# One tile pair per half head: a relu of a score difference on ScalarE, its add and maximum in one VectorE operation

## The reference

```python
mod = (_silu(L0_c) @ L0_wmod).reshape(L0_c.shape[0], 6, 1, -1)
h = _layernorm(x) * (1 + ca) + sa
q = ((h @ W_q + b_q) @ W_s)            # into heads of 16 columns
k, v = h @ W_k + b_k, h @ W_v + b_v
scores = einsum('bhqd,bhkd->bhqk', q, k) / sqrt(16)
out = einsum('bhqk,bhkd->bhqd', softmax(scores), v)
x = x + ga * (out @ W_o + b_o)
h = _layernorm(x) * (1 + cb) + sb
x = x + gb * ffn(h)                    # 8 experts, each takes its 512 best tokens
```

## Time and profile before

| | |
|---|---|
| median of three runs | 1736.55 us (1734.66 to 1736.87) |
| profiled execution | span 1734.7 us; mean granted TensorE clock 0.979 |
| attention's exponentials | 131 to 1397 us |
| a unit | 19.6 us in the even stretch |
| busy over the span | TensorE 97%, VectorE 87%, ScalarE 74%, GpSimd 13% |
| reduces of groups (L230) | 1024, 1191.6 us busy |
| exponentials (L1080) | 2048, 1079.4 us busy |
| group matmuls (L223), score matmuls (L584) | 2048 each |
| PV matmuls (L1139) | 10752 |

### The profile page before, as it was taken

The page is one execution under the profiler, slowest core; times in us unless marked ns, Lnnn a source line. Parts: engine busy times, 40 slices in busy tenths (PEclk is TensorE's granted clock), DMA queues, the critical chain, the costliest instruction groups (busy, mean ns, idle before and its releaser), DMA issues. The chain is left out here.

```text
span 1734.7 us, 43731 instructions
## 1 busy us (share of the span) xinstructions
PE 1685.5 (97%) x17251; PEld 969.8 (56%) x17251; DVE 1513.5 (87%) x1908; ACT 1291.7 (74%) x2454; POOL 229.3 (13%) x300
## 2 busy tenths in 40 slices
PE   8999999999999999999999999999999998599998
PEld 5645555555555555555555554555555586488887
DVE  5678999999999999999999999999999476687774
ACT  2327888888888888888888888888888834365663
POOL 0422012100010000001000000100000012135433
PEclk9999999999999999999999999999999997599999
DMA  8660443222222223323222223342220331235332
GB/s 265 207 178 24 92 98 53 41 41 39 52 55 39 41 49 52 47 40 65 41 42 39 39 41 54 59 60 39 41 42 12 108 107 61 98 101 143 89 82 37
DMA packets 93658, 122.03 MB, mean 70 GB/s; under 512 B 24060, under 2 KB 70716, under 8 KB 90348
## 3 DMA queue, kind: packets, MB, share of 16 engines
q1 hardware_dynamic: 84492, 109.22, 28.1%
q0 software_dynamic: 6144, 8.39, 2.7%
q10 hardware_dynamic: 2816, 1.61, 0.3%
HBM read 79.35 MB, written 38.54 MB: 68 GB/s over the span
## 5 line engine op out<-in xcount | busy, mean ns | idle before, releaser
L230 DVE TENSOR_REDUCE pmax<-ps 128x2 f32<-128x1024 f32 x1024 | 1191.6, 1215 | 54.2 <-PE ps L223 50.2
L1080 ACT ACTIVATE pt<-ps 128x512 f32<-128x512 f32 x2048 | 1079.4, 600 | 179.8 <-PE ps L584 157.7
L223 PE MATMUL ps<-kp,qp 48*128 48x512 f32 x2048 | 622.4, 458 | 2.9 <-DVE pmax L230 2.9
L1139 PE MATMUL ps<-pt,v_st 128*32 128x256 f32 (+1 forms) x10752 | 589.7, 334 | 0.7 <-ACT pt L1080 0.7
L584 PE MATMUL ps<-qp,kp 50*128 50x512 f32 x2048 | 560.8, 422 | 0.5 <-ACT pt L1080 0.5
L584 PEld LDWEIGHTS ps<-qp,kp 50*128 50x128 f32 x2048 | 292.5, 185 | 265.2 <-ACT pt L1080 263.1
L1139 PEld LDWEIGHTS ps<-pt,v_st 128*32 128x32 f32 x10752 | 265.7, 109 | 261.0 <-issue 187.2
L223 PEld LDWEIGHTS ps<-kp,qp 48*128 48x128 f32 x2048 | 245.6, 184 | 108.1 <-issue 89.8
L213 POOL CAST m_parts<-rowmax_t 128x32 fp32r<-128x32 f32 x64 | 13.5, 211 | 864.5 <-DVE rowmax_t L247 864.5
L1752 PE MATMUL ps<-w_l,hid_h 128*128 128x256 f32 x256 | 72.3, 283 | 0.0
L446 ACT ACTIVATE pt<-ps,xb 128x512 fp32r<-128x512 f32 x32 | 21.8, 687 | 64.7 <-PE ps L613 63.7
(11 more groups left out here) (229 smaller groups left out, 1297.6 us busy)
## 6 DMA issues: line engine op xcount, KB each, us to landing
kp<-k_parts SPq DMA_DIRECT2D x186, 128.0 KB, 4.5
v_all<-L_ffn_w SPq DMA_DIRECT2D x16, 1024.0 KB, 6.9
qp<-q_parts SPq DMA_DIRECT2D x186, 64.0 KB, 4.1
k_parts<-pt SPq DMA_DIRECT2D x16, 512.0 KB, 3.4
q_parts<-pt SPq DMA_DIRECT2D x16, 512.0 KB, 2.9
o_rows<-o_sb SPq DMA_DIRECT2D x64, 128.0 KB, 3.4
sums_c<-o_rows SPq DMA_DIRECT2D x512, 0.5 KB
m_rows<-m_parts SPq DMA_DIRECT2D x256, 2.0 KB
```

Of the source, the lines that this page charges most:

```text
L223: last = nc.tensor.matmul(slot[:, half * CH:(half + 1) * CH], qp[rows, r, a * P:(a + 1) * P], kp[rows, r, c * CH:(c + 1) * CH], start=True ...
L230: v.reduce_max(pmax[:, u % 2, 2 * k:2 * k + 2], slot.rearrange("p (f t) -> p f t", f=2), AX.X).then_inc(groups_out, 1)
L1080: nc.scalar.activation(pt[:, s % PTS, half * CH:(half + 1) * CH], bank(n % SCORE_BANKS), ACT.Exp, scale=SCALE).then_inc(scores_out, 1)
L1139: last = mm(acc[32 * j:32 * (j + 1), first * QB:(first + many) * QB], v_st[:, h % NBUF, kt, :], probs[:, :, j * QB:(j + 1) * QB], start=kt ...
```

## The change

For the units 2 to 61 (`folds`), the key chunks 2 and 3 of the last query tile (groups 14 and 15) are treated in another way. Group 14 is not made. TensorE makes instead, for each of the two halves, the difference of the two chunks' scores, in a bank of the score ring: queries times chunk 2, then, accumulated onto it, negated queries times chunk 3 (`fold_scores`). ScalarE writes the relu of that difference to `fold` (`take_fold`). Group 15 is filled as before with chunk 3's scores; VectorE adds the relu to them, which gives the larger of the two chunks' scores, and takes the maximum over the row in the same operation (`tensor_tensor_reduce`), one for each half.

The two fold products of unit u stand in the scores of unit u-1, ahead of its chunks 5 (low rows, block 1) and 6 (high rows, block 2). They take places in the ring of three banks (`RING`, `FOLD_RING`), so a unit has 34 places for 32. GpSimd negates the query tile (`negate_queries`) behind the split of the maxima of the unit before. Block 5 issues one group where it issued two, so that there are 15 in a unit. Waits that counted groups or chunks count by the new lists.

```diff
+LOWEST = -3.0e38
+FOLD_TILE, FOLD_FROM, FOLD_END = KT // NCH - 1, 2, UNITS - 2
+FOLD_K = FOLD_TILE * NCH + NCH - 1
+FOLD_PLACES = (5, 6)
+def folds(u):
+    return FOLD_FROM <= u < FOLD_END
+GROUPS = [(u, k) for u in range(UNITS) for k in range(KT) if not (folds(u) and k == FOLD_K - 1)]
+FOLD_BEFORE = {(u - 1) * UNIT_CHUNKS + at: (u, half) for u in range(FOLD_FROM, FOLD_END) for half, at in enumerate(FOLD_PLACES)}
+RING, FOLD_RING = [], {}
+for chunk in range(UNITS * UNIT_CHUNKS):
+    if chunk in FOLD_BEFORE:
+        FOLD_RING[FOLD_BEFORE[chunk]] = len(RING) + len(FOLD_RING)
+    RING.append(len(RING) + len(FOLD_RING))
...
+        q_minus = sb("q_minus", [P, P], F32R)
+        fold = stage_b[:, 0, :].rearrange("p (h t) -> p h t", h=2)
...
         def reduce_group(dve, v, n, slot):
-            u, k = divmod(n, KT)
+            u, k = GROUPS[n]
             dve.wait_ge(groups_full, n + 1)
-            v.reduce_max(pmax[:, u % 2, 2 * k:2 * k + 2], slot.rearrange("p (f t) -> p f t", f=2),
-                         AX.X).then_inc(groups_out, 1)
+            if folds(u) and k == FOLD_K:
+                if u < FOLD_FROM + 2:
+                    v.memset(pmax[:, u % 2, 2 * k - 2:2 * k], LOWEST)
+                for half in range(2):
+                    dve.wait_ge(scores_out, FOLD_RING[u, half] + 1)
+                    last = v.tensor_tensor_reduce(fold[:, half, :], slot[:, half * CH:(half + 1) * CH], fold[:, half, :],
+                                                  1.0, LOWEST, ALU.add, ALU.max,
+                                                  accum_out=pmax[:, u % 2, 2 * k + half:2 * k + half + 1])
+                last.then_inc(groups_out, 1)
+            else:
+                v.reduce_max(...)
...
+        def fold_scores(pe, u, half):
+            h, f = divmod(u, HALVES)
+            at, a = FOLD_RING[u, half], f * (QT // 2) + FOLD_TILE
+            rows = slice(HALF * half, HALF * half + KROWS)
+            pe.wait_ge(q_negated, u - FOLD_FROM + 1)
+            pe.wait_ge(scores_out, at - SCORE_BANKS + 1)
+            nc.tensor.matmul(ring_bank(at), qp[rows, h % NBUF, a * P:(a + 1) * P],
+                             kp[rows, h % NBUF, 2 * CH:3 * CH], start=True, stop=False)
+            nc.tensor.matmul(ring_bank(at), q_minus[rows, :],
+                             kp[rows, h % NBUF, 3 * CH:4 * CH], start=False, stop=True).then_inc(scores_full, 1)
+        def negate_queries(pool, g, u):
+            h, f = divmod(u, HALVES)
+            r, a = h % NBUF, f * (QT // 2) + FOLD_TILE
+            pool.wait_ge(operands_in[r], (h // NBUF + (r > 0)) * 16 * loads_of_head)
+            pool.wait_ge(parts_made, u)
+            if u > FOLD_FROM:
+                pool.wait_ge(scores_full, FOLD_RING[u - 1, 1] + 1)
+            for half in range(2):
+                rows = slice(HALF * half, HALF * half + KROWS)
+                links["pool"](g.tensor_scalar(q_minus[rows, :], qp[rows, r, a * P:(a + 1) * P].bitcast(F32), -1.0, None, ALU.mult))
+            pool.sem_inc(q_negated, 1)
         def scores(pe, s, half):
+            at = RING[n]
-            if n >= SCORE_BANKS:
-                pe.wait_ge(scores_out, n - SCORE_BANKS + 1)
+            if at >= SCORE_BANKS:
+                pe.wait_ge(scores_out, at - SCORE_BANKS + 1)
...
                     split_maxima(pool, g, u)
+                    if folds(u + 1):
+                        negate_queries(pool, g, u + 1)
...
+                def take_fold(u, half):
+                    act.wait_ge(scores_full, FOLD_RING[u, half] + 1)
+                    if u > FOLD_FROM:
+                        act.wait_ge(groups_out, GROUP_OF[u - 1, FOLD_K] + 1)
+                    nc.scalar.activation(fold[:, half, :], ring_bank(FOLD_RING[u, half]), ACT.Relu).then_inc(scores_out, 1)
                 for n in range(STEPS * 2):
+                    if n in FOLD_BEFORE:
+                        take_fold(*FOLD_BEFORE[n])
...
                     twice = b != DELAY and (b == 0 or b > DELAY and b % 2 == 1) or block == 2 * DELAY
+                    if b == BLOCKS // 2 and block > BLOCKS:
+                        twice = False
                     for n in range(many):
                         if n == (0 if twice or b == DELAY else 1) and group < len(GROUPS):
                             next_group(group)
                             group += 1
+                        if chunk in FOLD_BEFORE:
+                            fold_scores(pe, *FOLD_BEFORE[chunk])
                         scores(pe, *divmod(chunk, 2))
                         chunk += 1
```

More of the change, by code:

```diff
@@ L68 @@
 GATHER_SPARE = 14
+LOWEST = -3.0e38
[5 more added lines that the diff above has]
+GROUPS = [(u, k) for u in range(UNITS) for k in range(KT) if not (folds(u) and k == FOLD_K - 1)]
+GROUP_OF = {at: n for n, at in enumerate(GROUPS)}
+FOLD_BEFORE = {(u - 1) * UNIT_CHUNKS + at: (u, half) for u in range(FOLD_FROM, FOLD_END) for half, at in enumerate(FOLD_PLACES)}
[4 more added lines that the diff above has]
+    RING.append(len(RING) + len(FOLD_RING))
 class Link:
@@ L227, in reduce_group @@
         def reduce_group(dve, v, n, slot):
-            u, k = divmod(n, KT)
+            u, k = GROUPS[n]
             dve.wait_ge(groups_full, n + 1)
-            v.reduce_max(pmax[:, u % 2, 2 * k:2 * k + 2], slot.rearrange("p (f t) -> p f t", f=2),
-                         AX.X).then_inc(groups_out, 1)
+            if folds(u) and k == FOLD_K:
[8 more added lines that the diff above has]
+            else:
+                v.reduce_max(pmax[:, u % 2, 2 * k:2 * k + 2], slot.rearrange("p (f t) -> p f t", f=2),
+                             AX.X).then_inc(groups_out, 1)
             if k == 0 and u > 0:
                 join_maxima(dve, v, u - 1)
-            if n == STEPS - 1:
+            if n == len(GROUPS) - 1:
                 join_maxima(dve, v, u)
         def join_maxima(dve, v, u):
-            dve.wait_ge(groups_out, (u + 1) * KT)
+            dve.wait_ge(groups_out, GROUP_OF[u, KT - 1] + 1)
             if u > 0:
@@ L294, in adaln_moe_block @@
             GROUPS_OF[n] = ("u0", "u1", "u2", "u3", "t", "v0", "v1")
-        scores_full, scores_out = sem("scores_full"), sem("scores_out")
+        scores_full, scores_out, q_negated = sem("scores_full"), sem("scores_out"), sem("q_negated")
         def group_at(n, place):
@@ L569, in project_dve, with ring_bank @@
                     normalise(n + 2)
+        def ring_bank(at):
+            return bank(at % SCORE_BANKS)
+        def fold_scores(pe, u, half):
[19 more added lines that the diff above has]
+            pool.sem_inc(q_negated, 1)
         def scores(pe, s, half):
@@ L580, in scores @@
                 pe.wait_ge(low_done, chunks * 4 - 1)
-            if n >= SCORE_BANKS:
-                pe.wait_ge(scores_out, n - SCORE_BANKS + 1)
+            if at >= SCORE_BANKS:
+                pe.wait_ge(scores_out, at - SCORE_BANKS + 1)
             rows = slice(HALF * half, HALF * half + MROWS)
-            nc.tensor.matmul(bank(n % SCORE_BANKS), kp[rows, h % NBUF, kt * P:(kt + 1) * P],
+            nc.tensor.matmul(ring_bank(at), kp[rows, h % NBUF, kt * P:(kt + 1) * P],
                              qp[rows, h % NBUF, f * CH:(f + 1) * CH], start=True, stop=True).then_inc(scores_full, 1)
@@ L837, in project_rows @@
                 pe.wait_ge(xb_ready, 2 * NB)
-                pe.wait_ge(groups_out, STEPS)
+                pe.wait_ge(groups_out, len(GROUPS))
                 pe.wait_ge(normalised, G // HG // NB * HALVES)
@@ L933, in load_next @@
                 def load_next(g):
-                    sp.wait_ge(scores_full, (g + 1) * HALVES * KT * 2)
+                    sp.wait_ge(scores_full, RING[(g + 1) * HALVES * UNIT_CHUNKS - 1] + 1)
                     if g == 0:
@@ L1078, in _ @@
                         act.wait_ge(pv_done, blocks_until(n - 2 * PTS))
-                    act.wait_ge(scores_full, n + 1)
-                    nc.scalar.activation(pt[:, s % PTS, half * CH:(half + 1) * CH], bank(n % SCORE_BANKS),
+                    act.wait_ge(scores_full, RING[n] + 1)
+                    nc.scalar.activation(pt[:, s % PTS, half * CH:(half + 1) * CH], ring_bank(RING[n]),
                                          ACT.Exp, scale=SCALE).then_inc(scores_out, 1)
@@ L1091, in invert @@
                     inverse(v, f).then_inc(inverse_made, 1)
-                for n in range(EARLY_GROUPS, STEPS):
-                    u, k = divmod(n, KT)
+                for n in range(EARLY_GROUPS, len(GROUPS)):
+                    u, k = GROUPS[n]
                     done = u - 3
@@ L1131, in weigh @@
                     ready = chunks_of(block)
-                    pe.wait_ge(scores_out, ready[-1] + 1)
+                    pe.wait_ge(scores_out, RING[ready[-1]] + 1)
                     for s in sorted({n // 2 for n in ready}):
@@ L1153, in _ @@
                     twice = b != DELAY and (b == 0 or b > DELAY and b % 2 == 1) or block == 2 * DELAY
+                    if b == BLOCKS // 2 and block > BLOCKS:
```

(7 more changed lines are left out.)

## The result

The changed kernel takes 1801.66 us in the median of four runs (1800.21 to 1802.63), the one before 1736.01 (1734.66 to 1736.87): ratio 1.0384, 95% interval 1.0368 to 1.0399. It is slower by 65.7 us; 1804 was forecast. The profiled execution's span is 1800.8 us, 66.1 more. The sums carry differences and don't change by it.

The account below looks back on a forecast made before the run. TensorE and ScalarE, handing each other three PSUM banks, set the pace, not VectorE. Slots and bank waits sum to 1.15 us per unit, 69 us in 60 units, on 1734.7: 1803.7, said as 1804 (range 1758 to 1824).

Parts of the forecast that it names:

- PV behind the short block: PV matmuls after the block of chunks 6 and 7, where the second fold stands, come 1.20 us late.
- PV behind block 3: PV matmuls after the block of chunk 10, which waits for chunk 7's bank, come 1.39 us late.
- VectorE worth nothing: VectorE's two reduces become two adds with maximum, 0.8 us less busy per unit; worth nothing on the path.
- ScalarE's Relu at 0.49: Each of the two new 128x512 Relus per unit on ScalarE takes 0.49 us, as exps do start to start.
- Three slots more, one less: On TensorE, folds add three matmul slots per unit, block 5 loses one: two of 0.24, 0.48 us at least.
- The ring: Among three score banks, chunk 5 waits for chunk 3's exp, chunk 10 for chunk 7's: 0.67 us per unit beyond slots.
- Halves that overtake: On TensorE, chunk 6 may run beside the second fold's first product, one slot earlier: nothing or 14 us less.
- GpSimd: Negating the query tile twice per unit takes 0.3 us each, with cover of over 8 us before the fold.
- Rival 1: Only TensorE's added matmul slots cost time: 0.48 x 60 = 29 us, 1764; chance 0.15.
- Rival 2: Three matmuls in a row on one half leave TensorE's weight loads unhidden: 33 us more, 1837; chance 0.09.
- Rival 3: Extra matmuls and Relus fall in idle gaps, only block 5's slot counts: 14 us less, 1720; chance 0.09.
- Rival 4: Relu and Exp need different function tables on ScalarE, four switches per unit: 307 us, 2042; chance 0.01.

Follow-up runs that it names:

- the run that relieved it alone: Kernel before, with a memset in place of VectorE's reduce of group 14 in units 2 to 61: 1733.16 us, ratio 0.9992.
- the runs of single folds: Kernel after with one fold only, key chunk 2 left out for the other half: 1762.98 us with the first fold, 1758.21 with the second.
- slots alone: Kernel after without group 14, the four fold products issued into the next group's slot, with no ring place, Relu or negation: 1753.83 us.

## Why the prediction was right

Point by point, in its own steps; offsets are from the output copy of the unit shown.

| step | forecast | measured |
|---|---|---|
| chunk 5 | late by 0.71 (0.94 behind the copy) | 721.56 - 720.61 = 0.95 |
| PV behind it | late by 0.72 | 1.38 for 0.64: 0.74 |
| PV behind the short block | late by 1.20 | 3.08 for 1.87: 1.21 |
| PV behind block 3 | late by 1.39 | 5.24 for 3.83: 1.41 |
| PV to PV over the block of chunk 5 | 2.4 to 2.5 | 721.99 - 719.53 = 2.46 |
| block 5 | gives back 0.24 | 1.96 to 1.75: 0.21 |
| unit | 1.15 more, 20.8 | 1.14 more, 20.78 |
| 60 units | 69 | 68.5 |

PV to PV, in medians of the units, the block of chunk 5 grew by 0.69 (1.77 to 2.46; its PV is 0.73 later behind the copy, and the copy itself 0.04 earlier), the short block by 0.46 and block 3 by 0.20; block 5 gave 0.21 back. That is the 1.14.

The span grew by 66.1, 2.4 less than the units' sum. 1.4 of it lie behind the last copy (336.1 to 334.7), and 0.7 in one unit that took 20.37 us before and has the usual length now. What is left nearly cancels: the units at both ends grew by 0.7 less in all, and the first copy comes 0.5 later. None of it is in the forecast, which would be met at 1804 without it.

- *VectorE worth nothing.* Right, and shown by the run that relieved it alone. Two adds with maximum were to take 1.5 us; they take 1.3: 0.69 each, 0.61 to 0.62 start to start. Over the span VectorE's busy time fell by 43.9 us, forecast 46.
- *ScalarE's Relu at 0.49.* Right: 721.88 to 722.36. With no bias column it lasts 0.60, as an exp.
- *Three slots more, one less.* The count is right. What a slot costs depends on its place: 0.24 in the short block, nothing in the first fold, where the ring's stall covers it, and 0.14 there without a stall.
- *The ring.* Right in place and size. The one thing said amiss was that c3's exp is late because of the copy: ahead of chunk 2, with no copy, a fourth place costs more still. Chunk 10's wait is the one forecast: for chunk 7's exp, which comes late behind the second Relu.
- *Halves that overtake.* Chunk 6 ran beside the first product of the second fold (722.89, 722.90) and started ahead of the second (723.14), which is queued in front of it. The timeline had it beside the second, and the prediction held either possible. It moved nothing: the block ended late by 1.21 for 1.20.
- *GpSimd.* The negation was taken at 0.3 us and lasts 0.53, and the cover held it: nobody waited for it but its own queue, 0.7 us.
- *Rival 1*, slots alone (1764), falls with the runs of single folds and of slots alone. *Rival 2*, weight loads laid bare (1837): the first fold's products are 0.30 apart, 0.06 more than a slot, but in a stall, and the second's 0.24. *Rival 3*, faster (1720), needed the folds for nothing; without them the kernel runs at 1718. *Rival 4*, function tables: no switch, since the Relu and the next exp stand 0.48 apart; the trace has five table loads as before, none between 84.3 and 1464 us.

## What to carry to other kernels

An engine at 96% was not the bound here, since the others waited 2.9 us for it in 1110: look who waits for whom before taking work off it, and try the relief by itself, since one memset for a reduce would have shown zero. Work moved into the ring of three banks cost more than its duration, because one place more in a block of three chunks made the last of them wait for the block's first exp: 0.72 us here for a place whose exp takes 0.49 and whose products take 0.48. To price such a place, rewrite the unit's timeline with every bank's last reader; it gave the ends of the three blocks that got longer within 0.02 us here, where a count of slots gave 29 us of the 66.

## What was not expected of the hardware

- Two matmuls of 64 columns on rows that another matmul needs next cost the short block a whole slot (1.47 for 1.23 us), although they ran only 0.19 and 0.27 us, almost at once (711.64, 711.67).
- Taking work from VectorE alone changed its waits and nothing else to 0.003 us per unit.
- A product on the same 64 rows as the one before it starts 0.23 to 0.31 us behind it; the weights are loaded beside the running matmul even then (a load of 0.19 us from 720.96, beside the matmul that runs 0.46 us from 720.89).
